# When GpSimd sends its scatters in the late quads of an attention and expert kernel: seven waits per quad become two

## What is computed

```
xn = layernorm(x)                           # x: 8 x 1024 tokens x 128, float32
q, k, v = split(xn @ W_qkv)                 # 16 heads of 8; k layer-normed per head
y = causal linear attention in chunks of 64 tokens, state S += v k^T
attn = y @ W_o
expert(t) = argmax(xn[t] @ centroids.T)     # 8 experts
ffn(t) = gate * (w2 relu(w1 (norm(xn) * ln_g + ln_b) + b1) + b2) + xn   # of the token's expert
out = x + attn + ffn
```

## Time and profile before

| | us |
|---|---|
| median of 3 runs | 392.41 |
| lowest and highest run | 391.08, 395.75 |
| span of the profiled execution, first to last instruction | 363.3 |
| median less that span | 29.1 |

### The profile page before, as it was taken

One profiled execution on the slowest core, in us unless ns is written; L12 is line 12 of the kernel. 1 busy time (PEld: TensorE's weight loads), 2 busy tenths in 40 slices (PEclk: granted clock), 3 DMA queues, 4 the chain that ended last, 5 costly groups with the idle time before them and its releaser, 6 DMA issues.

```text
span 363.3 us, 17565 instructions
## 1 busy us (share of the span) xinstructions
PE 342.1 (94%) x6868; PEld 293.0 (81%) x6868; DVE 287.1 (79%) x799; ACT 241.8 (67%) x657; POOL 251.7 (69%) x245
## 2 busy tenths in 40 slices
PE   6799999998999999999999989999999999999991
PEld 6466786776787687777867879999999999999990
DVE  8888897898886888878877786788777788777860
ACT  4788687677587666757566735766666667666660
POOL 3488477789788765556455513888888888888884
PEclk9989999999999999999999999999999999999996
DMA  6220433636314021545553445555545555555420
GB/s 196 70 60 8 118 91 97 184 104 194 106 47 120 19 87 54 157 109 163 150 152 93 131 105 134 72 73 72 72 65 74 71 63 74 74 76 59 38 23 0
DMA packets 55153, 33.18 MB, mean 91 GB/s; under 512 B 5352, under 2 KB 52768, under 8 KB 55072
## 3 DMA queue, kind: packets, MB, share of 16 engines
q1 hardware_dynamic: 42800, 23.53, 23.9%
q0 software_dynamic: 12272, 8.54, 17.2%
HBM read 18.72 MB, written 13.78 MB: 89 GB/s over the span
## 4 chain that ended last, share of the span: by engine, by line
issue 25%; POOL 13%; PE 11%; DVE 1%; DMA 1%; POOLq 1%; ACT 1%; SPq 0%; DVEq 0%; ACTq 0%
POOL out_dram L494 13%; PE bank L1328 2%; PE sc L1274 2%; PE bank L1337 2%; PE bank L1222 1%; DMA out_dram<-res 1%; POOLq L71 1%; PE bank L1200 1%; PE bank L1306 1%; DVE pr L856 1%; PE bank L1209 1%; PE bank L1295 1%; PE bank L1255 1%; PE bank L1215 0%; PE bank L1233 0%
## 5 line engine op out<-in xcount | busy, mean ns | idle before, releaser
L494 POOL DMA_INDIRECT out_dram<-qx,rows x71 | 112.9, 1590 | 35.1 <-issue 22.1
L694 ACT ACTIVATE qx<-sc,b1T 128x128 f32<-128x128 f32 x280 | 79.8, 368 | 39.6 <-PE sc L1421 39.6
L420 POOL DMA_INDIRECT slots_d<-rows,pos_i x64 | 64.2, 1003 | 43.1 <-issue 11.0
L856 DVE TENSOR_TENSOR pr<-sc,causal 128x1536 f32<-128x1536 f32 (+2 forms) x33 | 63.6, 1929 | 17.4 <-PE sc L1274 17.2
L1429 PE MATMUL bank<-tokens,qx 128*128 128x128 f32 x568 | 75.3, 276 | 0.8 <-ACT qx L694 0.7
L1421 PE MATMUL sc<-wide,tokens 128*128 128x128 f32 x560 | 74.0, 275 | 0.2 <-issue 0.2
L1429 PEld LDWEIGHTS bank<-tokens,qx 128*128 128x128 f32 x568 | 69.0, 192 | 1.4 <-ACT qx L694 1.4
L1421 PEld LDWEIGHTS sc<-wide,tokens 128*128 128x128 f32 x560 | 68.1, 192 | 0.3 <-issue 0.3
L1015 DVE COPY tokens<-xT 128x1024 f32 x71 | 55.2, 778 | 0.0
L1274 PEld LDWEIGHTS sc<-qx,kT 32*64 32x64 f32 x2048 | 32.5, 132 | 16.4 <-issue 15.8
L1030 DVE SCALAR_TENSOR_TENSOR qx<-bank,rows,qx 128x128 f32<-128x128 f32 x71 | 24.9, 350 | 26.3 <-PE bank L1429 25.8
(11 more groups left out here) (167 smaller groups left out, 532.2 us busy)
## 6 DMA issues: line engine op xcount, KB each, us to landing
rows<-slots_d SPq DMA_DIRECT2D x71, 66.0 KB, 2.0
res<-in_L_attn_x_dram SPq DMA_DIRECT2D x16, 256.0 KB, 4.1
out_dram<-res SPq DMA_DIRECT2D x16, 256.0 KB, 3.4
tokens<-in_L_attn_x_dram SPq DMA_DIRECT2D x7, 512.0 KB, 4.2
w1raw<-in_L_ffn_w_dram SPq DMA_DIRECT2D x8, 256.0 KB, 4.0
w2raw<-in_L_ffn_w_dram SPq DMA_DIRECT2D x8, 256.0 KB, 4.3
out_dram<-qx,rows POOLq DMA_INDIRECT x71, 3.4
slots_d<-rows,pos_i POOLq DMA_INDIRECT x64
```

What stands on the lines that cost most here:

```text
L420: pool.indirect_dma_start(slots_d, bass.IndirectOffsetOnAxis(ap=pos_i[:, t:t + 1], axis=0), rows[:, t, :], None, bounds_check=E * RT * P - ...
L494: pool.indirect_dma_start(out_rows, bass.IndirectOffsetOnAxis(ap=xs[:, a, D + 2:D + 3].bitcast(U32), axis=0), ye[:, a, :], None, bounds_ch ...
L694: last = nc.scalar.activation(ht[:, k % 2, c * P:(c + 1) * P], inner(k)[:, c * P:(c + 1) * P], ACT.Relu, bias=b1T[:, bass.ds(e * FC + c, 1)])
L856: nc.vector.tensor_tensor(pr[:, h % 2, a:G, w].rearrange("p g (j t) -> p g j t", t=CH), sc[:, a * BANK:G * BANK].rearrange("p (g w) -> p g ...
```

## The change

GpSimd's list for quads 9 to 15 is written anew. Instead of seven waits with one scatter each, a quad has two waits: for the products of the half before (`av_ps` at 2n), then two scatters, and for the second scores (`sc_ps` at 2n+2), then five. The number of scatters in a quad (7) and their order stay. The last tile, 63, waits in quad 15 for `av_ps` at 30, the products L1328 of quad 14's second half; before, it waited for `sc_ps` at 31, the first scores of quad 15. `send_rows(2)` at the end sends one tile, since 63 have gone by then.

```
-            for h in range(ROUTED, NH):
-                n = h // 2
-
-                pool.wait_ge(s("sc_ps"), h + 1)
-                send_rows(1)
-                if h % 2 == 0:
-                    pool.wait_ge(s("av_ps"), h)
-                    send_rows(1)
-                    if n + 1 < NQ:
-                        pool.wait_ge(s("q_ps"), n + 2)
-                        send_rows(1)
-                elif n + 1 < NQ:
-                    pool.wait_ge(s("v_ps"), n + 2)
-                    send_rows(1)
-                    pool.wait_ge(s("out_ps"), n)
-                    send_rows(1)
-                    pool.wait_ge(s("w2_ps"), n - 6)
-                    send_rows(1)
+            for n in range(LATE, NQ - 1):
+
+                pool.wait_ge(s("av_ps"), 2 * n)
+                send_rows(2)
+
+                pool.wait_ge(s("sc_ps"), 2 * n + 2)
+                send_rows(5)
+            pool.wait_ge(s("av_ps"), 2 * (NQ - 1))
+            send_rows(2)
```

## The result

The kernel after took 406.53 us (median of 4 runs, 403.74 to 408.11) against 391.75 for before: a ratio of 1.035, with a 95% interval of 1.0275 to 1.043. By the medians that is 14.8 us more, where 1.1 was forecast.

What follows compares the result with a forecast made beforehand. TensorE was taken to bound the late quads, and the last scatters the end. Terms 0 + 0 + 1.06 us on a span of 363.3 gave 364.4, with 29.1 outside it 393.5 us; range 391.0 to 396.0.

Steps and rivals of the forecast that it cites:

- What bounds the kernel now: Late quads: TensorE sets the pace, busy 12.24 of 12.70 us; of the scatters only the last ones lie on the path.
- Outside the span: Whole run: 29.1 us taken to lie outside the profiled span, added to the forecast span of 364.4 to give 393.5.
- Part 1: Late quads, scatters regrouped as two and five: all fit, no engine waits for them, 0 us.
- do they fit: Quad 11: five scatters from 165.6 last until 172.0, against 171.96 before, so none is late and no backlog arises.
- Part 2: Late quads, scatters over VectorE's folds L897: contention taken as 0 to 0.4 us, at most 10.4 us.
- scatter first, fold second: VectorE's folds: an order the trace didn't refute, where by the skill's rule the fold would wait for the whole scatter.
- below nothing: Late quads: a gain can't exceed TensorE's present waits, 1.6 + 1.4 = 3.0 us; none of it was taken.
- Part 3: Last tile, quad 15: tile 63 starts 1.06 us later, delaying slot loads, stores and second stage by as much.
- Slower by contention: Rival, six late quads: a scatter holds up the first fold, passed on by L613; 6 us, 7 with last tile; chance 0.08.
- A fold over 350 ns: Sign of being wrong, VectorE in the late quads: L897 lasting over 350 ns, where 286 was expected.
- TensorE waits for L613: Sign of being wrong, seam between quads: TensorE waiting for ScalarE's weight copy by more than 0.5 us a quad.

Runs made afterwards that it cites:

- b0: The kernel before, unchanged, profiled again on the chip of the experiments: 390.81 us, span 389.1.
- e4: Against the kernel after, all 43 late scatters sent behind quad 14, none in quads 9 to 14: pitch 12.5 us a quad; total time not compared.
- e8: Against the kernel after, SyncE issues plain DMAs of the same rows, GpSimd's 43 scatters come behind the quads: pitch 13.0 us a quad.
- e14: Against the kernel after, GpSimd computes in the scatters' places, the 43 scatters come behind the quads: pitch 12.7 us a quad.
- e3: Against the kernel after, groups swapped: five scatters after the last products, two after the second scores; 413.96 us, ratio 1.057.
- e1: Against the kernel before, only the last tile's wait changed, to av_ps at 30: 392.65 us against 391.53, ratio 1.0025.
- e6: Against the kernel after, the five split: one after the second scores, four after the value projection; 405.29 us against 388.59, ratio 1.042 to before.
- e2: Against the kernel after, the last tile waits for sc_ps at 31 as before; groups of two and five stay: 404.85 us, ratio 1.034 to before.
- e9: Against the kernel before, scatters regrouped: two after first scores, one after last products, two after second scores, one after value projection, one after output; ratio 1.0025.
- e10: Against the kernel before, scatters regrouped: three after first scores, one after last products, two after second scores, one after value projection; ratio 1.017.
- e11: Against the kernel before, scatters regrouped: two after first scores, two after last products, two after second scores, one after value projection; ratio 0.9955.
- e15: Against the kernel before, scatters regrouped: two after first scores, two after last products, two after second scores, one after output; ratio 1.004.
- e12: Against the kernel after, one to six short scatters after second scores in quads 9 to 14, full ones behind: losses 0.3, 0.6, 3.8, 6.7, 5.4, 6.3 us.

## Why the prediction was wrong

**What bounds the kernel now** was right in naming TensorE, and wrong in the sentence "Moving them inside a quad can matter only through contention" as it was then used: the contention looked for was VectorE's. The rows of TensorE were read for what they waited for, and the profile had none of the effect in it.

**Outside the span.** The prediction took the 29.1 us between span and median as fixed. In b0 and after it is 1.7 us. The trace on which every row rests was thus of a course 23 us quicker than the quickest timed run of before (363.3 + 1.7 against 388.1), and the 29 us were the sign of it. The quads 4 to 8, the same in all kernels, take 66 us in it and 72 to 76 in the later traces. Seven scatters a quad cost nothing in that trace (pitch 12.6 against 12.5 in e4), so its rows had to give 0. Why that one execution escaped stays open; no run repeated it.

**A rival that no run tests** is that the recording of the trace has a part in the stops. ScalarE and VectorE update semaphores some 155 times in quads 9 to 14. In e4, e8 and e14, where no scatter goes out there, the trace has a record for each of them, within 5 us; in the first profile 3 are missing, in b0 34, in after 17, in e3 32. So the records go missing where scatters go out and TensorE stops, and hardly any do in the execution that escaped. Every run here has a span and a granted clock, so none ran unrecorded. Whether a scatter stops TensorE in this way when nothing is recorded isn't known.

**Part 1** (the same scatters at other places, 0 us) is the step that failed. The sum "do they fit" was right: GpSimd was idle before each group, and no scatter was late. But the 0.30 us between two scatters was taken as GpSimd's business alone. It measured 14.5 us over six quads: from quad 9's first scores to quad 15's, 248.27 - 141.12 = 107.15 us in after against 234.33 - 141.67 = 92.66 in b0. In place of 0 stand TensorE's own stops and late increments while scatters follow one another. Of the 14.1 us between the late windows of after and b0, 9.0 are idle time of TensorE (18.3 against 9.3), and 5.1 are longer busy time (90.9 against 85.8), at a granted clock of 0.91 in place of 1.00.

**Part 2.** The folds, L888 in after, went as taken: a median of 286 ns and at most 355 in the 28 of the late quads, this being the group of that line.

```profile
L888 DVE SCALAR_TENSOR_TENSOR w1raw<-w1raw,lbb x28: 280/286/355, 147.0 to 248.2; 128x128 f32<-128x128 f32 x28
```

Eleven of them begin while a scatter is under way and last 280 to 292 ns; those above 293 ns are ones inside which a scatter begins. So the order scatter first, fold second, which the prediction left open, doesn't block the fold for a scatter's length. The first profile had that order too, in nine of its 28 folds, and the prediction overlooked it:

```profile
138.83 1.08 POOL L420 DMA_INDIRECT slots_d<-rows,pos_i  x1 [1.32 <-PE bank L1200]
```
```profile
139.21 0.28 DVE L897 SCALAR_TENSOR_TENSOR w1raw<-w1raw,lbb 128x128 f32<-128x128 f32 x1
```

By the rule of the Trainium skill weighed there ("SBUF — State Buffer", "Who interferes with whom") as the prediction applied it, the shared ports were the danger, and the trace disagrees: 0.07 us at most. That section of the Trainium skill also lets TensorE wait for nobody on its SBUF ports; whether these are the path here no run shows. The bound "below nothing", 3.0 us, missed the 2.9 us a quad that seven scatters cost in b0.

**Part 3** (the last tile, 1.06 us) held in its sum, as far as it can be told. The timed runs of e1 (+1.1 us) don't set it apart from nothing. The traces do better: from quad 15's first scores to the end it is 155.2 to 156.2 us in the four with the new wait (after, e1, e3, e6; mean 155.8) and 154.3 to 155.5 in the seven with the old one (first profile, b0, e2, e9, e10, e11, e15; mean 154.7). Its terms were off. SyncE begins the slot loads 7.0 us after those scores (255.28 - 248.3) in place of 4.4 (238.67 - 234.3), later by 2.6; the eight loads then take 4.99 us instead of 5.94, and the first output scatter is 0.8 us later (264.86 - 248.3 against 250.03 - 234.3). SyncE in after, with the end of the chain, to be held against the earlier trace rows:

```profile
255.28 4.99 SPq L330 DMA_DIRECT2D rows<-slots_d  x8
260.32 0.98 SPq L299 DMA_DIRECT2D out_dram<-res  x2
```
```profile
260.80 3.18 DMA out_dram<-res
```

**The rivals.** "Slower by contention" had the side, the seam at L613 and, at 7 us, half the size, but VectorE's fold as the place. A fold over 350 ns came once in 28 (355), and b0 has one of 361. The prediction's list of what would prove it wrong had "TensorE waits for L613", and that didn't come either: 1.0 us in all six quads of after, matmuls and weight loads together. What the list lacked is TensorE stopping by itself.

**Shown and not shown.** Shown: the late quads lose time to indirect DMAs of GpSimd (2.9 us a quad in b0), and what after loses beyond that comes from runs of them that begin some 1.3 us after one another; not from their bytes, their rows, or the same rows sent by plain DMAs. That GpSimd's being busy as such isn't the cause is shown for short computations only. By what path the scatters stop TensorE's instructions and hold its increments stays open, and so does the part of the recording.

## What to carry to other kernels

Scatters on an otherwise idle GpSimd aren't free: look at what TensorE does within the next microseconds of each, above all where it runs many short matmuls. Waits that seem idle can be spacing; before merging them, count how many indirect DMAs then begin 0.3 us after one another, and keep such runs at one or two; here that only avoided a loss and brought next to no gain. And when a profile's span and the timed runs differ by more than a couple of microseconds, take a second profile before believing any row.

## What the hardware showed unexpectedly

A semaphore increment of TensorE can come long after its matmul's recorded end: 4.4 to 5.9 us for `v_ps` under five scatters, about 1.2 us for scores and products in b0. A run of three or more short scatters 1.27 us apart cost a quad 3.8 to 6.7 us, one or two 0.3 to 0.6 (e12, one quad each). In such a stretch TensorE did 4, 5 and 9 matmuls at a time, one such batch every 0.76 us (186.05, 186.80, 187.56 in b0). A cut from 128 rows to 32 shortens a scatter from 0.97 to 0.87 us only.
